# A graph network on one Trainium2 core: constant TensorE products in the third edge stage and in the score stage

## The chip, the cores and the metric

The kernel runs on one core of a Trainium2 chip. The metric is the device time of one execution in microseconds (us). Engines are named as in the profile: PE is TensorE, DVE VectorE, ACT ScalarE, POOL GpSimd, SP SyncE.

## What is computed

Four graph layers, one after the other, on 3125 nodes of 64 features and 103125 edges sorted by their target node. Each layer normalises the nodes, computes something for every edge from its source node, sums over the edges of each target node, and adds the result to the nodes. The parts that matter here are the third layer and the scores of the fourth:

```python
# third layer
he = mlp(edge_z, edge_ln, edge_W, edge_b)           # 64 -> 32 for each edge
msg = concatenate([hn[src], he])                    # 64 for each edge
emb_edge = mlp(msg, red_ln, red_W, red_b)           # layernorm, product, leaky relu
msg_sum = segment_sum(emb_edge, dst) + emb_local
z = msg_sum / (deg + 1)
# fourth layer, its scores
s = leaky_relu(gl[src] + gr[dst])                   # 6 heads of 64
e = einsum('ehf,hf->eh', s, att)
```

## The kernel before

The edges stand in tiles of 128, and 8 tiles are a batch of 1024 edges; 101 batches are in use. The layers are stages that follow one another, each with a loop over the batches in which the engines run side by side and hand work to each other with semaphores, in an order written out by hand. The stages that the change touches are `edge1` (second edge stage, its first instructions only), `edge2` (third edge stage) and `edge3a` (score stage).

**Third edge stage.** Batch number modulo 4 gives its slot. For slots 0, 1 and 2 the 1024 source rows are fetched by GpSimd with 8 indirect DMAs (`Gather.gather`, L892) into the tile `cat` of that slot. For slot 3 (`TAKEN`) nothing is gathered: TensorE selects the rows with one-hot matrices that VectorE makes (`hot`, L1827), in two bursts of 13 products of 128x512 (`choose`, L1683). The first burst is issued in the batch of slot 2, the second in that of slot 3.

For a batch of slots 0 to 2 TensorE (`body`, L1702 to L1750) waits for the gathered rows and for the edge half of `cat` (VectorE, L1853), transposes `cat` into the PSUM tile `catTp` (L1720; in the profile `edge_cat_t_ps`), computes the edge product of the next batch (`edge_part`, L1668), waits until ScalarE has copied `catTp` to SBUF (L1779), multiplies (L1736), and sums the messages of the batch before (`sum_up`, L1676). VectorE adds these sums to the node accumulator (L1875) and makes one-hots between the additions. `by_bank` is another name of `catTp`. The semaphore that counts finished transposes is also the one GpSimd waits for before it starts to gather the next batch of the same slot, four batches further on (`self.free` in `Gather.gather`):

```python
        wait_past(pool, self.free, 2 * t + h - 1)
...
        for j in range(B):
            nc.gpsimd.indirect_dma_start(
```

So one gather of 8 indirect DMAs starts after the transposes of each batch of slots 0, 1 and 2, and none after those of slot 3.

**Score stage.** Here GpSimd gathers all batches in the same manner, again released by the turning of a batch. TensorE does for batch n: `project(n, h, 0)` and `(n, h, 1)` (the first burst of L2040, 8 entries in the timeline), then `turn` of batch n+1 (L2031, L2032, into `hcTp`), `turn_scores` (L2047), and `project` 2 and 3 (second burst). ScalarE copies `hcTp` to SBUF (L2079) once both the turned batch n+1 and the products of batch n are there; VectorE weighs and sums the products (L2133, L2141).

**Start of the second edge stage.** VectorE's `run_marks` reads small PSUM results of TensorE; then its loop begins with a one-hot (L1526). TensorE's first instruction after its last small product is `sums(0, 0, 0)` (L1443).

Of the kernel before, what the change touches and what calls it, by code (L numbers as in the profile page):

```python
# [30 lines left out]
P = 128  # L31
# [133 lines left out]
def behind_one(t, q, m, h):  # L165

    return (t, 1, q, m) if h == 0 else (t + 1, 0, 1 - q, m + q)
# [30 lines left out]
def wait_past(engine, sem, value):  # L198

    if not isinstance(value, int) or value > 0:  # L200
        engine.wait_ge(sem, value)


def over(ap, n):
# [1116 lines left out]
def edge1(nc, k):  # L1321
# [3 lines left out]
    with Ctx(nc, "edge1_") as c:  # L1325
# [12 lines left out]
        rowsTp = c.ps("src_rows_t_ps", [P, ROWS])  # L1338
        row = c.ps("columns_ps", [P, 1, P])
        row_ready = c.sem("columns_in_psum")  # L1340
        ids = c.sb("dst_seq", [P, TILES + 2], I32)
        src = c.sb("src_seq", [P, TILES], I32)
        loop = c.sb("loop", [P, TILES])
# [16 lines left out]
        with nc.Block() as block:  # L1360
# [47 lines left out]
            def _(pe):  # L1408
# [28 lines left out]
                def sums(gi, v, p):  # L1437
                    n, h = GROUP * gi + p, p % 2
                    pe.wait_ge(msg_ready, n + 1)
                    pe.wait_ge(oh_ready, n + 1)  # L1440
                    wait_past(pe, added[B - 1], n - 1)
                    for j in range(B):
                        mm = pe.matmul(sp_[h][j % 2 * D:(j % 2 + 1) * D, j // 2, :], msg[h][:, j, :],  # L1443
                                       oh[h][:, j, :], start=True, stop=True)
                    mm.then_inc(sums_ready, 1)
# [6 lines left out]
                for i in range(3):  # L1452
# [2 lines left out]
                pe.wait_ge(count_ready, 1)  # L1455
                pe.matmul(marks[:, 3 * P:3 * P + 1], carry_t[:, :], k.ident[0:1, 0:1], start=True,
                          stop=True).then_inc(count_turned, 1)
                sums(0, 0, 0)

                def body(u):  # L1460
# [54 lines left out]
            @block.vector  # L1515
            def _(dve):
                def hot(gi, v, u, b):

                    if b == 0:
                        dve.wait_ge(srcb_loaded[v], 16 * (u + 1))  # L1520
                    wait_past(dve, hot_used, NB * gi + b + 1 - RING)
                    dve.tensor_scalar(ring[b % RING][:, :], srcb[v][:, :], k.node_col[:, b:b + 1], None,  # L1522
                                      ALU.is_equal).then_inc(hot_ready, 1)

                def onehot_of(n, h):
                    dve.tensor_tensor(oh[h][:, :, :], over(k.dst_rel[:, bass.ds(n * B, B)], P),  # L1526
                                      row[:, :, :].to_broadcast([P, B, P]), ALU.is_equal).then_inc(oh_ready, 1)

                def add(n, h, j, base):
                    if j > 1:  # L1530
                        dve.wait_ge(added[j - 2], n + 1)
                    else:
                        wait_past(dve, added[B - 2 + j], n)
                    half = slice(j % 2 * D, (j % 2 + 1) * D)
                    acc = k.acc_both[half, bass.ds(base, P)]
                    dve.tensor_tensor(acc, acc, sp_[h][half, j // 2, :], ALU.add).then_inc(added[j], 1)

                dve.wait_ge(high_ready, 1)
                dve.scalar_tensor_tensor(h16[:, :, D:2 * D], k.h[:, :, :], LIFT, h16[:, :, 0:D], ALU.mult,
                                         ALU.subtract).then_inc(prepared, 1)  # L1540
                for b in range(NB):
                    hot(0, 0, 0, b)
                dve.tensor_copy(row[:, 0, :], k.row0[:, :]).then_inc(row_ready, 1)
                dve.wait_ge(row_ready, 1)
                onehot_of(0, 0)
                onehot_of(1, 1)
                dve.memset(k.acc_both, 0.0).then_inc(prepared, 1)
                dve.wait_ge(prepared, 2)
                run_marks(dve, k, ids, src, loop, turn, counts_t, carry_t, carry, marks, Chain(dve, marks_step),
                          seq_loaded, marks_ready, marks_turned, count_ready, count_turned)  # L1550

                def body(u):
                    for v in (0, 1):
                        gi = 2 * u + v
                        for p in range(GROUP):
                            n, h = GROUP * gi + p, p % 2
                            b0, b1 = PART[p]
                            ahead = live(GROUP * gi + GROUP + TAKEN)
                            if not live(n):
                                continue  # L1560
                            dve.wait_ge(sums_ready, n + 1)
                            if live(n + 2):
                                onehot_of(n + 2, h)
                            for j, base in enumerate(batch_starts(nc, k, DVE, n)):
                                add(n, h, j, base)
                                if ahead and b0 + j < b1:
                                    hot(gi + 1, 1 - v, u + v, b0 + j)
                by_groups(dve, body)


def edge2(nc, k, cat, ga, catTp_ready):


    with Ctx(nc, "edge2_") as c:
# [43 lines left out]
        with nc.Block() as block:  # L1618
# [42 lines left out]
            def _(pe):  # L1661
# [10 lines left out]
                def sum_up(n, h):  # L1672
                    pe.wait_ge(msg_ready, n)
                    pe.wait_ge(oh_ready, n)
                    for j in range(B):
                        mm = pe.matmul(sums[:, j, :], msg[h][:, j, :], oh[h][:, j, :], start=True, stop=True)  # L1676
                    mm.then_inc(sums_ready, 1)
# [28 lines left out]
                def body(t, q, m):  # L1706
                    first = isinstance(t, int) and t == 0
                    for h in (0, 1):
# [34 lines left out]
                        if not (first and h == 0):  # L1743
                            if not (first and h == 1):
                                pe.wait_ge(added[B - 1], n)
                            sum_up(n - 1, 1 - h)
                by_parity(pe, body)
                pe.wait_ge(added[B - 1], USED + 1)
                sum_up(USED, 0)
# [170 lines left out]
def edge3a(nc, k):  # L1920
# [3 lines left out]
    with Ctx(nc, "edge3a_") as c:  # L1924
# [25 lines left out]
        with nc.Block() as block:  # L1950
# [67 lines left out]
            def _(pe):  # L2018
# [33 lines left out]
                def body(t, q, m):  # L2052
                    first = isinstance(t, int) and t == 0
                    for h in (0, 1):
                        if not used_batch(t, h):
                            continue
                        n = 2 * t + h + 1
                        pe.wait_ge(hcT_ready, n + 1)
                        project(n, h, 0)
                        project(n, h, 1)  # L2060
                        if used_batch(t, h + 1):
                            tt, hh, qq, mm = behind_one(t, q, m, h)
                            turn(n + 1, hh, tt + 1, qq, mm)
                        if not (first and h == 0):
                            turn_scores(n - 1, 1 - h)
                        project(n, h, 2)
                        project(n, h, 3)
# [427 lines left out]
def build(nc, ins, out):  # L2495
# [15 lines left out]
    with Ctx(nc) as c:  # L2511
# [68 lines left out]
        with Ctx(nc, "layers_") as layers:  # L2580
# [6 lines left out]
            k.before, k.behind, k.kept_before, k.kept_behind, k.times = (  # L2587
                layers.sb(name, [P, TILES]) for name in (
                    "run_before", "run_behind", "kept_before", "kept_behind", "times"))
            k.flags_t = layers.sb("flags_t", [SIDES2, 2, P])  # L2590
            edge1(nc, k)
            with Ctx(nc, "table2_") as shared:
# [89 lines left out]
```

## Time and profile before

| | us |
|---|---|
| median of 3 runs (lowest, highest) | 6671.85 (6656.55, 6678.16) |
| the profiled execution, its time | 6677.32 |
| its span | 6675.1 |
| PE busy | 4704.2 (70%) |
| DVE busy | 4170.2 (62%) |
| POOL busy | 3155.2 (47%) |
| ACT busy | 1888.7 (28%) |
| mean granted TensorE clock | 0.829 of full |
| third edge stage, 3330 to 4576 | 1246.0 |
| score stage, 4671 to 5905 | 1234.0 |

The two stage lines are stretches of the span, in us from its start, with 101 batches each, that is 12.3 and 12.2 us a batch. Busy times are sums over an engine's instructions; the granted clock is the share of the full TensorE clock that the chip granted. A timeline line gives the start, the duration, the engine, the source line, the operation with its output and inputs, how many instructions were put together, and in brackets the idle time of the engine before them with the work that is taken to have ended it.

### The profile page before, as it was taken

To read this page: it belongs to the slowest core of one execution; us is meant where nothing else is said; L and a number is where in the kernel's file an instruction comes from. 1 tells how busy PE (TensorE), PEld (TensorE's weight loads), DVE (VectorE), ACT (ScalarE), POOL (GpSimd) and SP (SyncE) were. 2 spreads that over 40 slices of the span, in tenths; PEclk is the share of its full clock that TensorE was granted. 3 is DMA by queue.
4 is the path that set the end of the run, shared out by engine and by line. 5 is a ranking of instruction groups with operands and counts; after the bars stand their busy time and mean duration, and the time that the engine had idled before them with its cause. 6 is when DMAs were issued, how large, how long until landed. Compare 5 with 4: busy or idle time off the path is not lost. (4 is left out here: it accounts for less than half of the span.)

```text
span 6675.1 us, 100965 instructions
## 1 busy us (share of the span) xinstructions
PE 4704.2 (70%) x28624; PEld 3007.3 (45%) x28624; DVE 4170.2 (62%) x7653; ACT 1888.7 (28%) x6318; POOL 3155.2 (47%) x2946
## 2 busy tenths in 40 slices
PE   3777777777777676667566666663777777739998
PEld 2333333333334333333344554452444444418997
DVE  4454444444446666666666666664666766688997
ACT  1333333333333000000133333331000000016775
POOL 3433343333331655555354454452666666515554
PEclk7778787888888788888677878886999888869999
DMA  3222222222221111111111111111443334411111
GB/s 84 55 54 51 53 56 52 52 51 54 55 54 32 38 38 38 39 39 36 26 41 38 41 40 38 41 40 32 108 111 108 110 110 117 110 49 51 49 49 34
DMA packets 492408, 379.08 MB, mean 57 GB/s; under 512 B 345930, under 2 KB 378971, under 8 KB 492339
## 3 DMA queue, kind: packets, MB, share of 16 engines
q1 hardware_dynamic: 394803, 288.65, 15.3%
q0 software_dynamic: 90560, 83.37, 7.0%
q10 hardware_dynamic: 6976, 6.23, 0.3%
q8 instruction: 33, 0.54, 0.0%
q14 instruction: 36, 0.29, 0.0%
HBM read 341.76 MB, written 36.12 MB: 57 GB/s over the span
## 5 line engine op out<-in xcount | busy, mean ns | idle before, releaser
L1009 POOL DMA_INDIRECT edge_src_rows<-table_wh,edge_gather_idx x806 | 787.1, 977 | 1169.5 <-DVE edge_small L1128 924.6
L1038 PE MATMUL edge_sums_ps<-edge_onehot_src,edge_halves 128*128 128x512 bf16 x4840 | 1048.3, 361 | 302.5 <-issue 296.5
L892 POOL DMA_INDIRECT edge3a_src_rows<-table_h,edge3a_gather_idx x808 | 764.3, 946 | 564.1 <-issue 311.2
L2040 PE MATMUL edge3a_z_ps<-Wz,edge3a_both_ends_t 128*128 128x396 f32 x1616 | 695.3, 579 | 365.2 <-DVE edge3a_terms L2133 315.1
L1114 DVE TENSOR_SCALAR edge_onehot_src<-layer_node_row,edge_src_col,edge_magnitude 128x1568 bf16<-128x1568 f16 x605 | 410.5, 679 | 842.8 <-remote 471.6
L892 POOL DMA_INDIRECT table_cat<-table_hn,table_gather_idx x592 | 599.5, 1013 | 631.6 <-PE edge_cat_t_ps L1720 340.4
L1401 POOL DMA_INDIRECT edge_src_rows<-table_h,edge_gather_idx x608 | 606.9, 998 | 553.9 <-PE edge_msg_ps L1433 190.8
L1038 PEld LDWEIGHTS edge_sums_ps<-edge_onehot_src,edge_halves 128*128 128x128 f16 x4840 | 428.0, 104 | 872.7 <-issue 537.7
L2133 DVE SCALAR_TENSOR_TENSOR edge3a_terms<-edge3a_z_ps,att_z 128x792 f32<-128x792 f32 x404 | 386.0, 977 | 406.1 <-DMA edge_edge_attr<-in_ea 223.9
L2040 PEld LDWEIGHTS edge3a_z_ps<-Wz,edge3a_both_ends_t 128*128 128x128 f32 x1616 | 333.5, 217 | 670.1 <-DVE edge3a_terms L2133 359.6
L2452 PE MATMUL edge3b_sums_ps<-edge3b_onehot,edge3b_weighted 128*128 128x128 f32 x4848 | 572.7, 278 | 6.2 <-DVE layers_accT L2490 4.5
L2452 PEld LDWEIGHTS edge3b_sums_ps<-edge3b_onehot,edge3b_weighted 128*128 128x128 f32 x4848 | 553.5, 193 | 11.8 <-DVE layers_accT L2490 4.7
L1416 PE MATMUL edge_src_rows_t_ps<-edge_onehot_src,edge_h_halves 128*128 128x512 f16 x1300 | 375.1, 431 | 230.4 <-DVE edge_onehot_src L1522 149.2
L2369 POOL TENSOR_TENSOR edge3b_weighted<-edge3b_src_rows,edge3b_alpha 128x1920 f32<-128x1920 f32 x101 | 350.3, 3468 | 344.9 <-DVE edge3b_alpha L2469 251.2
L2418 ACT ACTIVATE edge3b_weighted<-edge3b_src_rows,edge3b_alpha 128x64 f32<-128x64 f32 x1818 | 445.1, 334 | 166.1 <-DVE edge3b_alpha L2469 157.3
L1736 PE MATMUL edge_msg_ps<-rR,edge_cat_t 64*128 64x128 f32 x1616 | 180.7, 388 | 371.8 <-DVE edge_u L1861 255.4
L1066 ACT ACTIVATE edge_dst_rows<-edge_dst_rows_ps 128x390 f32<-128x390 f32 x153 | 70.4, 460 | 1293.1 <-DMA scores_by_head<-setup_zeros 928.5
L2079 ACT ACTIVATE edge3a_both_ends_t<-edge3a_both_ends_t_ps 128x1024 f32<-128x1024 f32 x101 | 103.5, 1024 | 1161.9 <-DMA edge_edge_attr<-in_ea 690.4
L1038 PE MATMUL edge_sums_ps<-edge_onehot_src_act,edge_halves 128*128 128x512 bf16 x1608 | 336.6, 340 | 77.0 <-issue 76.6
L2141 DVE TENSOR_REDUCE edge3a_scores<-edge3a_terms 128x24 f32<-128x1584 f32 x202 | 364.5, 1805 | 7.0
L1023 PE MATMUL edge_dst_rows_ps<-edge_window,edge_onehot_t 128*128 128x65 f32 x1632 | 263.0, 314 | 121.8 <-issue 82.8
L1875 DVE TENSOR_TENSOR layers_accT<-layers_accT,edge_sums_ps 65x128 f32 x808 | 198.7, 280 | 236.7 <-remote 217.7
(372 smaller groups left out, 8320.9 us busy)
## 6 DMA issues: line engine op xcount, KB each, us to landing
edge_dst_row<-in_dst_row SPq DMA_DIRECT2D x102, 512.0 KB
edge3a_dst_row<-in_dst_row SPq DMA_DIRECT2D x102, 512.0 KB
edge_window<-table_wh SPq DMA_DIRECT2D x816, 32.5 KB
edge3a_window<-table_h SPq DMA_DIRECT2D x816, 32.0 KB
edge_edge_attr<-in_ea SPq DMA_DIRECT2D x101, 256.0 KB
kept_rows<-edge3a_src_rows SPq DMA_DIRECT2D x101, 256.0 KB
edge3b_src_rows<-kept_rows SPq DMA_DIRECT2D x101, 256.0 KB
edge_edge_attr<-in_ea SPq DMA_DIRECT2D x101, 128.0 KB
```

The lines of the kernel that those rows point to most:

```text
L892: nc.gpsimd.indirect_dma_start(self.slot(b, j), None, self.table[:, :], bass.IndirectOffsetOnAxis(ap=self.idx[b][:, j:j + 1], axis=0)).the ...
L1009: nc.gpsimd.indirect_dma_start(g[q][:, j, :], None, k.t_wh[:, :], bass.IndirectOffsetOnAxis(ap=idx[q][:, j:j + 1], axis=0)).then_inc(gathe ...
L1038: mm = pe.matmul(acc[:, i, 0:w], halves[q][:, j, a, :, :].rearrange("p h d -> p (h d)"), hot[:, o:o + w], start=first and a == 0, stop=False)
L1114: dve.tensor_scalar(slot_v(q, j)[:, :], k.node_row[:, :], col[q][:, j:j + 1], mag[q][:, j:j + 1], ALU.is_equal, ALU.mult).then_inc(hot_v, 1)
L1401: nc.gpsimd.indirect_dma_start(g[p][:, j, :], None, k.t_h[:, :], bass.IndirectOffsetOnAxis(ap=idx[p][:, j:j + 1], axis=0)).then_inc(gather ...
L1416: mm = pe.matmul(rowsTp[:, o:o + 512], h16[:, b, :], ring[b % RING][:, o:o + 512], start=(b == 0), stop=(b == NB - 1))
L2040: mm = pe.matmul(zp[q % 2][:, i, 0:H * ZH], hcT[h][:, j * P:(j + 1) * P], k.Wz[:, :], start=True, stop=True)
L2133: dve.scalar_tensor_tensor(terms[:, 2 * q:2 * q + 2, :], zp[q % 2][:, :, 0:H * ZH], 0.0, rows_over(k.att_z[:, :], 2), ALU.max, ALU.mult).t ...
L2141: dve.tensor_reduce(scs[h][:, :, j:j + B // 2].rearrange("p h b -> p b h"), terms[:, j:j + B // 2, :].rearrange("p b (h f) -> p b h f", h= ...
L2369: return engine.tensor_tensor(hp[h][:, a:b, :, :], rows, weights, ALU.mult)
L2418: w = act.activation(hp[h][:, j, a, :], st[h][:, j, :], ACT.Copy, scale=al[h][:, a, j:j + 1])
L2452: mm = pe.matmul(sums[j % 4][:, i, :], hp[h][:, j, 2 * i:2 * i + 2, :].rearrange("p a d -> p (a d)"), oh[h][:, j, :], start=True, stop=True)
```

## The change

A function `spin` issues products of a constant fp16 matrix of 128x128 with a constant fp16 matrix of 128x512. Nobody reads the results. The third edge stage issues 10 of them at the end of each batch, except the batch of slot 2, into the bank of `catTp` (76 times). The score stage issues 6 between `project(n, h, 1)` and `turn` of the next batch, into the first bank of `hcTp` (100 times). The constants are a new SBUF tile `fill`, written once by VectorE at the start of the second edge stage, where TensorE waits for that with a new semaphore.

```diff
+def spin(pe, k, out, times):
+
+    for _ in range(times):
+        pe.matmul(out, k.fill[:, 0:P], k.fill[:, :], start=True, stop=True)
...
+        marks_free = c.sem("marks_read")
...
                 pe.matmul(marks[:, 3 * P:3 * P + 1], carry_t[:, :], k.ident[0:1, 0:1], start=True,
                           stop=True).then_inc(count_turned, 1)
+                pe.wait_ge(marks_free, 1)
                 sums(0, 0, 0)
...
                           seq_loaded, marks_ready, marks_turned, count_ready, count_turned)
+                dve.memset(k.fill[:, :], 1.0).then_inc(marks_free, 1)
...
                             if not (first and h == 1):
                                 pe.wait_ge(added[B - 1], n)
                             sum_up(n - 1, 1 - h)
+                        if b != TAKEN - 1:
+                            spin(pe, k, by_bank, 10)
...
                         project(n, h, 1)
                         if used_batch(t, h + 1):
                             tt, hh, qq, mm = behind_one(t, q, m, h)
+                            spin(pe, k, hcTp[:, 0:512], 6)
                             turn(n + 1, hh, tt + 1, qq, mm)
...
+            k.fill = layers.sb("fill", [P, 512], F16)
```

In the changed kernel the lines of the third edge stage are numbered 9 higher and those of the score stage 11 higher; the new products have line L207. The instructions of ACT, POOL and SP stand as they did.

TensorE in the loop of the third edge stage, before: the end of one batch, the next batch's transposes into `edge_cat_t_ps`, and that batch up to its sums.

```order
L1736 MATMUL edge_msg_ps<-rR,edge_cat_t 128x128 x8
L1676 MATMUL edge_sums_ps<-edge_onehot,edge_msg 65x128 x8
L1716 REGISTER_ALU
L1717 ISA
L1720 MATMUL edge_cat_t_ps<-ident,table_cat 128x128 x4
L1668 MATMUL edge_he_ps<-eR,edge_edge_attr 128x96 x8
L1736 MATMUL edge_msg_ps<-rR,edge_cat_t 128x128 x8
L1676 MATMUL edge_sums_ps<-edge_onehot,edge_msg 65x128 x8
L1717 REGISTER_ALU
L1720 MATMUL edge_cat_t_ps<-ident,table_cat 128x128 x4
```

The same place with the change.

```order
L1745 MATMUL edge_msg_ps<-rR,edge_cat_t 128x128 x8
L1685 MATMUL edge_sums_ps<-edge_onehot,edge_msg 65x128 x8
L207 MATMUL edge_cat_t_ps<-layers_fill 128x512 x10
L1725 REGISTER_ALU
L1726 ISA
L1729 MATMUL edge_cat_t_ps<-ident,table_cat 128x128 x4
L1677 MATMUL edge_he_ps<-eR,edge_edge_attr 128x96 x8
L1745 MATMUL edge_msg_ps<-rR,edge_cat_t 128x128 x8
L1685 MATMUL edge_sums_ps<-edge_onehot,edge_msg 65x128 x8
L207 MATMUL edge_cat_t_ps<-layers_fill 128x512 x10
```

The 10 products stand between a batch's sums and the wait (ISA) for the next batch's gathered rows, ahead of its transposes.

TensorE in the score stage, before: the end of one turning, the second burst of a batch and the first of the next (4 products each, in one line), and the next turning.

```order
L2032 MATMUL edge3a_both_ends_t_ps<-ident,edge3a_src_rows 64x128
L2047 MATMUL edge3a_scores_t_ps<-ident,edge3a_scores 48x128
L2040 MATMUL edge3a_z_ps<-Wz,edge3a_both_ends_t 128x396 x8
L2031 MATMUL edge3a_both_ends_t_ps<-edge3a_onehot_t,edge3a_window 64x128
L2032 MATMUL edge3a_both_ends_t_ps<-ident,edge3a_src_rows 64x128
L2031 MATMUL edge3a_both_ends_t_ps<-edge3a_onehot_t,edge3a_window 64x128
```

The same place with the change.

```order
L2043 MATMUL edge3a_both_ends_t_ps<-ident,edge3a_src_rows 64x128
L2058 MATMUL edge3a_scores_t_ps<-ident,edge3a_scores 48x128
L2051 MATMUL edge3a_z_ps<-Wz,edge3a_both_ends_t 128x396 x8
L207 MATMUL edge3a_both_ends_t_ps<-layers_fill 128x512 x6
L2042 MATMUL edge3a_both_ends_t_ps<-edge3a_onehot_t,edge3a_window 64x128
L2043 MATMUL edge3a_both_ends_t_ps<-ident,edge3a_src_rows 64x128
L2042 MATMUL edge3a_both_ends_t_ps<-edge3a_onehot_t,edge3a_window 64x128
```

The 6 products stand behind the first burst and ahead of the turning of the next batch.

## Rows read from the trace of the kernel before

**Rows 1.** Busy time by stretch: third edge stage, then score stage. Columns in the first line.

```profile
core 0: us, PE busy (x) PEld busy (x) DVE busy (x) ACT busy (x) POOL busy (x), PEclk, DMA share, GB/s
3330.00:4576.00 1246.00, 804.28 (x5998) 619.75 (x5998) 809.25 (x2162) 459.64 (x3501) 591.65 (x585) 0.80 0.16 38
4671.00:5905.00 1234.00, 899.85 (x5016) 526.93 (x5015) 857.37 (x803) 118.08 (x200) 733.39 (x776) 0.90 0.40 110
```

**Rows 2.** Waits of the third edge stage: who waited, for whom, us, times, longest.

```profile
POOL table_cat L892 <- PE edge_cat_t_ps L1720: 340.4, 26, 15.2
```

**Rows 3.** Timeline, TensorE: start, us, engine, line, operation; idle before in brackets.

```profile
3928.04 1.96 PE L1676 MATMUL edge_sums_ps<-edge_onehot,edge_msg 128*65 128x128 f32 x16
...
3930.60 0.66 PE L1720 MATMUL edge_cat_t_ps<-ident,table_cat 128*128 128x128 f32 x4 [0.60 <-DVE table_cat L1853]
...
3938.27 3.19 PE L1676 MATMUL edge_sums_ps<-edge_onehot,edge_msg 128*65 128x128 f32 x16
...
3941.29 0.60 PE L1720 MATMUL edge_cat_t_ps<-ident,table_cat 128*128 128x128 f32 x4
```

**Rows 4.** Timeline, TensorE, the batch of slot 1 that follows.

```profile
3954.49 0.60 PE L1720 MATMUL edge_cat_t_ps<-ident,table_cat 128*128 128x128 f32 x4
```

**Rows 5.** Timeline, GpSimd: gathers of the same stretch.

```profile
3932.05 1.67 POOL L892 DMA_INDIRECT table_cat<-table_hn,table_gather_idx  x1 [15.09 <-PE edge_cat_t_ps L1720]
...
3941.53 0.95 POOL L892 DMA_INDIRECT table_cat<-table_hn,table_gather_idx  x1 [0.30 <-issue]
...
3944.73 0.95 POOL L892 DMA_INDIRECT table_cat<-table_hn,table_gather_idx  x1 [2.25 <-issue]
...
3957.21 0.95 POOL L892 DMA_INDIRECT table_cat<-table_hn,table_gather_idx  x1 [2.16 <-PE edge_cat_t_ps L1720]
```

**Rows 6.** Timeline, VectorE, same stretch.

```profile
3944.75 0.28 DVE L1875 TENSOR_TENSOR layers_accT<-layers_accT,edge_sums_ps 65x128 f32 x1 [4.51 <-remote]
```

**Rows 7.** Timeline, TensorE, the same place one cycle later.

```profile
3987.13 2.67 PE L1676 MATMUL edge_sums_ps<-edge_onehot,edge_msg 128*65 128x128 f32 x16
```

**Rows 8.** Timeline, GpSimd, one cycle later: first and last gather of eight.

```profile
3980.93 1.67 POOL L892 DMA_INDIRECT table_cat<-table_hn,table_gather_idx  x1 [13.70 <-PE edge_cat_t_ps L1720]
...
3991.43 0.95 POOL L892 DMA_INDIRECT table_cat<-table_hn,table_gather_idx  x1 [0.31 <-issue]
```

**Rows 9.** Timeline, VectorE, one cycle later.

```profile
3994.74 0.28 DVE L1875 TENSOR_TENSOR layers_accT<-layers_accT,edge_sums_ps 65x128 f32 x1 [5.62 <-remote]
```

**Rows 10.** Timeline, TensorE: a second selection burst, partly at half clock.

```profile
3919.15 4.60 PE L1683 MATMUL edge_cat_t_ps<-edge_onehot_src,edge_node_parts 128*128 128x512 f16 x13 [1.98 <-DVE edge_src_rows_t L1837]
```

**Rows 11.** Timeline, TensorE: a second selection burst at full clock.

```profile
3668.99 2.98 PE L1683 MATMUL edge_cat_t_ps<-edge_onehot_src,edge_node_parts 128*128 128x512 f16 x13 [1.36 <-DVE edge_src_rows_t L1837]
```

**Rows 12.** Timeline, ScalarE, score stage.

```profile
4915.32 1.02 ACT L2079 ACTIVATE edge3a_both_ends_t<-edge3a_both_ends_t_ps 128x1024 f32<-128x1024 f32 x1 [11.04 <-DMA edge_edge_attr<-in_ea]
...
4927.40 1.02 ACT L2079 ACTIVATE edge3a_both_ends_t<-edge3a_both_ends_t_ps 128x1024 f32<-128x1024 f32 x1 [10.90 <-PE edge3a_z_ps L2040]
...
4939.45 1.02 ACT L2079 ACTIVATE edge3a_both_ends_t<-edge3a_both_ends_t_ps 128x1024 f32<-128x1024 f32 x1 [10.88 <-DMA edge_edge_attr<-in_ea]
```

**Rows 13.** Timeline, TensorE, score stage: the two bursts of a batch, the first of the next.

```profile
4916.48 4.62 PE L2040 MATMUL edge3a_z_ps<-Wz,edge3a_both_ends_t 128*128 128x396 f32 x8 [4.30 <-DVE edge3a_terms L2133]
...
4923.14 2.93 PE L2040 MATMUL edge3a_z_ps<-Wz,edge3a_both_ends_t 128*128 128x396 f32 x8
...
4928.56 2.92 PE L2040 MATMUL edge3a_z_ps<-Wz,edge3a_both_ends_t 128*128 128x396 f32 x8 [2.50 <-DVE edge3a_terms L2133]
```

**Rows 14.** Timeline, GpSimd, score stage: last gather of eight.

```profile
4924.80 0.95 POOL L892 DMA_INDIRECT edge3a_src_rows<-table_h,edge3a_gather_idx  x1 [0.30 <-issue]
```

**Rows 15.** Timeline, VectorE, start of the second edge stage.

```profile
2168.44 2.83 DVE L1547 MEMSET layers_accT<- 128x3328 f32 x1 [0.64 <-issue]
...
2191.93 1.22 DVE L1526 TENSOR_TENSOR edge_onehot<-dst_rel,edge_columns_ps 128x1024 f32<-128x1024 f32 x1
```

**Rows 16.** Timeline, TensorE, start of the second edge stage.

```profile
2188.24 1.97 PE L1443 MATMUL edge_sums_ps<-edge_onehot,edge_msg 128*64 128x128 f32 x32
```
## The prediction

> **What bounds the kernel now.** I read the windows of the two changed stages first. Neither is full of TensorE work: in the third edge stage TensorE is busy 804.28 of 1246 us, VectorE 809.25, GpSimd 591.65, at a granted clock of 0.80; in the score stage 899.85, 857.37 and 733.39 of 1234, at 0.90 [rows 1]. So waits set the time, and the question is whose. The table of waits shows GpSimd waiting for the transposes of L1720 340.4 us in 26 waits, up to 15.2 us each [rows 2]. 26 is the number of groups of four batches: GpSimd pauses once in each, where the batch of slot 3 brings it no gather. So I read one such cycle in the timelines.
>
> TensorE ends the sums of slot 3 at 3929.99 (3928.04 + 1.96) and starts the transposes of slot 0 at 3930.60, after only 0.60 us for the edge half made by VectorE [rows 3]. They end at 3931.26, and GpSimd starts its 8 gathers 0.79 later, at 3932.05 [rows 5]. That pair sets the pace of what follows: the last of the 8 ends at 3942.48 (3941.53 + 0.95) [rows 5]. TensorE's next sums ended at 3941.46 (3938.27 + 3.19) [rows 3], but VectorE, which adds them, resumes only at 3944.75, after 4.51 us idle [rows 6]; the transposes of slot 1 ended at 3941.89 [rows 3], and GpSimd, free since 3942.48, starts the next gather at 3944.73 [rows 5]. Both start some 2.3 us after the last gather's end. One cycle later the gathers run from 3980.93 and end at 3992.38 (3991.43 + 0.95) [rows 8], TensorE's sums end at 3989.80 [rows 7], and VectorE resumes at 3994.74 [rows 9], 2.36 after the gathers' end and 4.94 after TensorE's. The two distances to the gathers agree (2.27, 2.36), those to TensorE do not (3.29, 4.94). I choose the reading that, while a gather of 8 is running, what TensorE finishes is seen by the others only behind the last gather. The chain then goes: transposes of slot 0, gather, release, next gather. TensorE's clock is no part of it.
>
> **The change, part by part.** *One product* of the new kind is 128x512 in fp16, as the 13 of L1683. At full clock 13 take 2.98 us [rows 11]; with 0.38 for the last one to drain (my estimate, between 0 and the 0.66 that all 4 transposes take [rows 3]) each adds (2.98 - 0.38) / 12 = 0.217. So 10 take 2.17 and 6 take 1.30. Partly at half clock 13 take 4.60 [rows 10], so 10 are at most 3.54.
>
> *Third edge stage, slot 3, 25 times.* The 10 products start where the sums end, 3929.99, and end at 3932.16. TensorE idled 0.60 there; the transposes move by 2.17 - 0.60 = +1.57, and GpSimd's pause grows by it, 13.70 to 15.09 us already [rows 5, 8], so it had long been ready. 25 x 1.57 = **+39**. Bounds: all of 2.17 (25 x 2.17 = +54) if the cover of 0.60 is VectorE waiting in turn, and 0 if the later batches of the cycle return it.
>
> *Slot 0, 25 times.* The transposes of slot 1 ended at 3941.89, the release came some 2.0 later. 2.17 more fit to within 0.2; I take +0.1 each, **+2**, from 0 to +5. Name the cover: it is the gather, and it moves with the slot 3 delay.
>
> *Slot 1, 25 times.* Transposes end at 3955.09 (3954.49 + 0.60, no idle time ahead) [rows 4], GpSimd starts at 3957.21, by then idle 2.16 [rows 5]. With 2.17 they end at 3957.26, and with the 0.79 of above GpSimd starts at 3958.05: +0.84. In cycles where the sums are shorter (the 2.67 of rows 7 against 3.19 in rows 3) part of it fits. I take +0.4 each, **+10**, from 0 to +21.
>
> *Slot 2* has no products. Its batch and that of slot 3 hold the two selection bursts, which stand on the chain: GpSimd is in its long pause then. The second takes 4.60 in one cycle and 2.98 in another, 1.62 less [rows 10, 11]. I counted it slow in 13 of 25 cycles; if the products made all of them fast, 13 x 1.62 = -21. But the burst comes a whole batch after the nearest products, with 1.98 and 1.36 us of idle time directly ahead of it in the two cases, and that wait, for VectorE, is not shortened. I take **0**, from -21 to +19 (the other 12 slow).
>
> *VectorE in slot 0* makes its one-hots beside the first gather (1.67 instead of 0.95 [rows 5, 8]). It moves along; 0.
>
> *Score stage, 100 times.* The batch with a first burst of 4.62 and the next with 2.92 [rows 13] take 12.08 and 12.05 from one copy by ScalarE to the next [rows 12]. So 1.7 us of TensorE time moves the period by 0.03: here too the gathers hold it. The last of 8 ends at 4925.75 (4924.80 + 0.95) [rows 14], ScalarE copies at 4927.40 [rows 12], 1.65 later, while TensorE's second burst had ended at 4926.07 (4923.14 + 2.93) [rows 13]. The slack is 1.33 in the slow case and 1.7 more in the fast one; 1.30 fits in both, just. **0**, from -2 (the 0.03) to +9 (some 10 bursts that are slower still, 0.9 each, an estimate). The cover is the gather; without it 6 products would cost their whole length.
>
> *Second edge stage, once.* TensorE issued its 32 entries of two batches from 2188.24 [rows 16]; now they wait for VectorE, whose first one-hot starts at 2191.93 [rows 15], plus the memset: 2.83 us for 3328 columns [rows 15] gives 0.44 for 512. What TensorE does there, half of 1.97, is 0.99. **+1**, from 0 to +2.
>
> Sum: 39 + 2 + 10 + 0 + 0 + 1 = **+52** on the profiled execution's 6677.3, 6729. The median of the runs is 5.5 lower, so I predict 6724.
>
> **Where a rule speaks the other way.** The rows show TensorE idle in every batch of the score stage (4.30 and 2.50 ahead of the first burst) and the same burst at 4.62 or 2.92 [rows 13]: clock 1.2 GHz for part of it, then 2.4. The Trainium skill, page "TensorE: Matmul & The Clock Gate", says that idle gaps between bursts cost clock and that TensorE should be kept fed. The trace agrees that the clock is lost behind idle time; it doesn't agree that time is lost by it here, since 4.62 and 2.92 give one period. By the rule the change should be faster, which is rival C.
>
> **The rivals.**
> A, the forecast: the products of slot 3 delay the chain, the rest is covered. Chance 0.62.
> B, returned: the products raise the clock enough that the selection bursts all take 2.98 (-21), and slot 1 costs nothing; 39 + 2 + 1 - 21 = +21 with the rest at 0, and about +10 if the first burst gains too. Against it: the idle time ahead of the bursts. Around 6687. Chance 0.17.
> C, faster: TensorE, not the gathers, releases the batches. Then a first burst of 2.92 instead of 4.62 in some 60 score batches is 60 x 1.7 = -102, with -21 for the selection bursts and +39 + 1: -83, 6589. It decides at one point: whether ScalarE's copy follows TensorE's second burst or the last gather. Rows 12 to 14 speak for the gather. A lesser form, the selection bursts alone gaining in both batches with the delay of slot 3 swallowed, gives -30, 6642. Chance 0.10.
> D, slower by much: the 6 products don't fit in the 1.33 us, or what TensorE posts late misses one release and waits for a later one. 100 x 1.30 = +130 with the +52: 6854. Against it the slack, for it that it is only just enough. Chance 0.07.
> E, the products do not raise the clock at all (constant data, or the throttle sees them otherwise). The sum of A hardly changes, as no term of it is a gain, but 10 products at half clock take up to 3.54 instead of 2.17: 25 x 1.37 = +34 more, 6758. Chance 0.04.
>
> **How the numbers follow.** A measurement of this kernel can tell about 0.3% from no change, 20 us. A has its own range, 6690 to 6760, from its bounds; a few us of it lie under 6692. Faster by over 0.3% is C: 0.10. Within 0.3% is most of B and the low edge of A: 0.17. Slower: 0.73. The range of 8 in 10 takes A and B with E: 6670 to 6765; C and D stay out.
>
> **What would show it.** Right: in the third edge stage the 10 products (L207) behind the sums of slot 3, the transposes of slot 0 starting some 1.6 us later against VectorE's edge half, GpSimd's waits for L1729 some 40 us longer in sum, the stage 1298 instead of 1246 us; the score stage at 1234 still, with a higher granted clock. Wrong: if the score stage gets shorter, TensorE set its period; if the third stage stays at 1246, the delay of slot 3 was returned within the cycle, and my reading of the release falls; if the score stage grows by 60 us or more, the slack was no slack.

## The result: 6719 us, and the profile after

| | before | after |
|---|---|---|
| median of 5 runs each (lowest, highest), us | 6671.85 (6650.61, 6678.16) | 6719.28 (6705.97, 6737.4) |
| span of the profiled execution, us | 6675.1 | 6717.1 |
| third edge stage: first L1736 (after: L1745) to last, us | 1244.6 | 1271.2 |
| score stage: first L2040 (after: L2051) to last, us | 1234.8 | 1257.1 |
| mean granted clock | 0.829 | 0.843 |

The ratio is 1.0078, 95% interval 1.0057 to 1.0098: slower by 47 us. The prediction was 6724, in the range 6670 to 6765. The sum came out; its terms did not all. Of the 42 us of the two spans 26.6 lie in the third edge stage, where +51 was forecast, and 22.3 in the score stage, where 0 was. The rest, -7, is what other stretches differ by.

One thing has to be said before the experiments. They ran on three chips (numbers 4, 7 and 15), and there the kernel before takes 5230 us, not 6672 (5224 to 5242 in 73 runs). The record names no chip for the runs of the table, so it isn't known whether another chip, another setting or the recording of the traces makes the difference. The program is the same. "First condition" (6672 us) and "second condition" (5230 us) name the two below, and the difference between them turned out to be the most instructive part of this case.

The windows of the changed kernel's two stages, in the columns of their first line, stand against [rows 1].

```profile
core 0: us, PE busy (x) PEld busy (x) DVE busy (x) ACT busy (x) POOL busy (x), PEclk, DMA share, GB/s
3327.00:4598.00 1271.00, 957.81 (x6736) 689.94 (x6736) 806.31 (x2158) 460.94 (x3500) 585.44 (x584) 0.83 0.16 38
4690.00:5947.00 1257.00, 1040.59 (x5616) 568.82 (x5615) 857.28 (x804) 117.97 (x200) 731.37 (x776) 0.94 0.40 108
```

TensorE is busier (958 instead of 804 us, 1041 instead of 900), the clock is up by 0.03 and 0.04, and both stages are longer. The higher clock did not make either stage shorter here.

The same place of the third edge stage as in [rows 3], TensorE's timeline with the change:

```profile
3932.49 1.96 PE L1685 MATMUL edge_sums_ps<-edge_onehot,edge_msg 128*65 128x128 f32 x16
...
3934.29 2.32 PE L207 MATMUL edge_cat_t_ps<-layers_fill 128*128 128x512 f16 x10
...
3936.44 0.60 PE L1729 MATMUL edge_cat_t_ps<-ident,table_cat 128*128 128x128 f32 x4
...
3947.65 0.60 PE L1729 MATMUL edge_cat_t_ps<-ident,table_cat 128*128 128x128 f32 x4
```

The 10 products start behind the sums of slot 3, and the transposes come 1.99 us behind the end of the sums (3934.45), not 0.60. GpSimd, which answers to [rows 5], starts 0.79 later, as before:

```profile
3937.83 0.94 POOL L898 DMA_INDIRECT table_cat<-table_hn,table_gather_idx  x1 [15.21 <-PE edge_cat_t_ps L1729]
...
3946.97 0.94 POOL L898 DMA_INDIRECT table_cat<-table_hn,table_gather_idx  x1 [0.30 <-issue]
...
3950.25 0.94 POOL L898 DMA_INDIRECT table_cat<-table_hn,table_gather_idx  x1 [2.34 <-issue]
```

Its pause behind the last gather is 2.34 us, where [rows 5] has 2.25. In the table of waits its line has grown from 340.4 us in 26 waits to 407.6 in 44 [rows 2]:

```profile
POOL table_cat L898 <- PE edge_cat_t_ps L1729: 407.6, 44, 16.7
```

In the score stage something new stands in TensorE's timeline. First the burst, the 6 products, and the second burst, which is in pieces:

```profile
4927.89 4.62 PE L2051 MATMUL edge3a_z_ps<-Wz,edge3a_both_ends_t 128*128 128x396 f32 x8 [1.66 <-DVE edge3a_terms L2145]
...
4932.34 1.46 PE L207 MATMUL edge3a_both_ends_t_ps<-layers_fill 128*128 128x512 f16 x6
...
4935.84 0.93 PE L2051 MATMUL edge3a_z_ps<-Wz,edge3a_both_ends_t 128*128 128x396 f32 x2
...
4937.26 1.21 PE L2051 MATMUL edge3a_z_ps<-Wz,edge3a_both_ends_t 128*128 128x396 f32 x2 [0.49 <-issue]
...
4938.69 4.38 PE L2051 MATMUL edge3a_z_ps<-Wz,edge3a_both_ends_t 128*128 128x396 f32 x12 [0.21 <-issue]
```

Then the gathers (first and last of eight) and ScalarE's copies of the same batch:

```profile
4927.39 0.94 POOL L898 DMA_INDIRECT edge3a_src_rows<-table_h,edge3a_gather_idx  x1 [2.58 <-DMA edge_edge_attr<-in_ea]
...
4936.12 0.94 POOL L898 DMA_INDIRECT edge3a_src_rows<-table_h,edge3a_gather_idx  x1 [0.30 <-issue]
```

```profile
4926.72 1.02 ACT L2091 ACTIVATE edge3a_both_ends_t<-edge3a_both_ends_t_ps 128x1024 f32<-128x1024 f32 x1 [11.54 <-PE edge3a_z_ps L2051]
...
4938.99 1.02 ACT L2091 ACTIVATE edge3a_both_ends_t<-edge3a_both_ends_t_ps 128x1024 f32<-128x1024 f32 x1 [11.10 <-PE edge3a_z_ps L2051]
```

The second burst, 8 entries in 2.93 us in [rows 13], starts at 4935.84 and hands out 2 entries, then 2 more 1.4 us later, and the rest runs into the next first burst (12 entries in one row). ScalarE copies 1.93 us behind the last gather (4937.06), where it was 1.65 [rows 12, 14], and the batch takes 12.27 us instead of 12.05 to 12.08.

Does time or a number run out here? An entry is one instruction of those that a line of the timeline puts together. A batch of the kernel before has exactly 50 product entries (16 in the two bursts, 32 in the turning, 2 for the scores); with the change it has 56. Over the whole stage with the change, 78 of 86 gathers of eight have a gap of over 0.15 us in TensorE's work, in 76 of them after 47 to 53 entries counted from the start of the gathers, and that can be 7.0, 8.5 or 9.9 us after it. Batches with the gap take 12.34 us in the median, the eight without it 12.15 (a few of over 13 us left out). In the kernel before only 8 of 85 have such a gap, after 48 to 51 entries, and a batch takes 12.13. So a number fits better than a time: TensorE gets some 50 entries ahead while gathers run, and behind that an entry comes every 0.7 to 0.8 us. 0.2 us in nine of ten batches is some 18 of the stage's 22 us (an estimate from these medians). This is a reading of the traces; no run made in this condition varied the number. And the number isn't the same everywhere: in the third edge stage with the change TensorE begins 54 to 61 entries before its gap in 21 gathers, and 62 without one in 22.

What the prediction took for the rule, that everything TensorE finishes during a gather is seen only behind it, is not what these traces show. ScalarE, TensorE and ScalarE again, third edge stage of the kernel before, with gathers running from 3932.05 to 3942.48 [rows 5]:

```profile
3932.38 0.22 ACT L1756 ACTIVATE edge_squares<-edge_he_ps 128x64 f32<-128x64 f32 x1 [0.48 <-PE edge_he_ps L1668]
...
3936.26 2.08 PE L1736 MATMUL edge_msg_ps<-rR,edge_cat_t 64*128 64x128 f32 x16 [3.92 <-DVE edge_u L1861]
...
3938.37 0.23 ACT L1756 ACTIVATE edge_squares<-edge_msg_ps 128x64 f32<-128x64 f32 x1 [3.91 <-PE edge_msg_ps L1736]
...
3943.99 0.60 ACT L1779 ACTIVATE edge_cat_t<-edge_cat_t_ps 128x512 f32<-128x512 f32 x1 [2.74 <-DMA edge_gather_idx<-in_src_t]
```

TensorE ends L1736 at 3938.34, and ScalarE takes the result up 0.03 us later, in the middle of the gathers. Over the stage ScalarE does so while the gathers still run in 71 of 72 cases, in 27 of them within 0.1 us and in the others up to 3.7 us late. VectorE in the score stage, with gathers from 4916.04 to 4925.75 and the first burst ending at 4921.10 [rows 13, 14]:

```profile
4919.10 0.98 DVE L2133 SCALAR_TENSOR_TENSOR edge3a_terms<-edge3a_z_ps,att_z 128x792 f32<-128x792 f32 x1
...
4921.13 0.98 DVE L2133 SCALAR_TENSOR_TENSOR edge3a_terms<-edge3a_z_ps,att_z 128x792 f32<-128x792 f32 x1 [0.97 <-issue]
```

What comes late is what TensorE finishes later in a gather. Its sums end 5 to 10 us into one, and VectorE starts to add them only 2.04 to 2.45 us behind the last gather in all 51 cases. The transposes that end at 3941.89 reach ScalarE at 3943.99, 1.51 us behind the gathers. These late results are the ones that the prediction's chain uses, so its terms could be right although its rule is too wide.

At the start of the second edge stage, VectorE and then TensorE:

```profile
2162.34 2.83 DVE L1555 MEMSET layers_accT<- 128x3328 f32 x1 [0.65 <-issue]
...
2186.13 0.48 DVE L1559 MEMSET layers_fill<- 128x512 f16 x1 [0.17 <-DVE layers_times L1324]
```

```profile
2186.67 3.68 PE L1450 MATMUL edge_sums_ps<-edge_onehot,edge_msg 128*64 128x128 f32 x32 [4.29 <-DVE layers_fill L1559]
```

The memset takes 0.48, where 0.44 was estimated. From the first memset to the sums there are 24.33 us now and were 19.80 [rows 15, 16], and the 32 entries take 3.68 instead of 1.97, right behind 4.29 us in which TensorE idled. VectorE's first one-hot comes 2.86 us later, not 1.

### The profile page after: what moved, and what is told of

It is laid out like the page before. It is cut to its first block and busy times, and to the rows that moved or that the text cites. A ratio compares the mean times of both kernels' runs of the same rounds, so it can differ in the third digit from the quotient of the medians.

```text
span 6717.1 us, 103685 instructions
## 1 busy us (share of the span) xinstructions
PE 4989.6 (74%) x29984; PEld 3116.7 (46%) x29984; DVE 4170.8 (62%) x7654; ACT 1890.7 (28%) x6318; POOL 3142.5 (47%) x2946
## 5 line engine op out<-in xcount | busy, mean ns | idle before, releaser
L898 POOL DMA_INDIRECT table_cat<-table_hn,table_gather_idx x592 | 594.1, 1004 | 664.9 <-PE edge_cat_t_ps L1729 407.6
L2051 PE MATMUL edge3a_z_ps<-Wz,edge3a_both_ends_t 128*128 128x396 f32 x1616 | 702.3, 559 | 239.8 <-issue 115.9
L2051 PEld LDWEIGHTS edge3a_z_ps<-Wz,edge3a_both_ends_t 128*128 128x128 f32 x1616 | 316.1, 207 | 580.6 <-issue 297.4
L1745 PE MATMUL edge_msg_ps<-rR,edge_cat_t 64*128 64x128 f32 x1616 | 170.0, 370 | 261.4 <-DVE edge_u L1872 191.1
```

Source lines behind the costliest of these rows:

```text
L898: nc.gpsimd.indirect_dma_start(self.slot(b, j), None, self.table[:, :], bass.IndirectOffsetOnAxis(ap=self.idx[b][:, j:j + 1], axis=0)).the ...
L2051: mm = pe.matmul(zp[q % 2][:, i, 0:H * ZH], hcT[h][:, j * P:(j + 1) * P], k.Wz[:, :], start=True, stop=True)
```

## The experiments

Eleven kernels ran, all in the second condition, each with a profile, beside the kernel before on the same chip. Where a kernel has products, the fill tile and the new wait are in it too.

### The kernel before again

> The kernel before, unaltered, for its trace. If it takes 5236 us again: in the third edge stage the gathers of slots 0, 1 and 2 follow each other 1.25 us apart without a pause, and VectorE takes up TensorE's sums within 0.1 us of their end, while a gather runs. If it takes 6672: as in the profile of before, with pauses of 2.2 us between the gathers.

5230.64 us, ratio 1.0004 (0.9994 to 1.0015). Its windows for the two stages:

```profile
core 0: us, PE busy (x) PEld busy (x) DVE busy (x) ACT busy (x) POOL busy (x), PEclk, DMA share, GB/s
2365.00:3384.00 1019.00, 717.77 (x5990) 579.97 (x5988) 805.56 (x2159) 463.08 (x3500) 579.54 (x584) 0.88 0.20 47
3450.00:4457.00 1007.00, 816.73 (x5016) 509.17 (x5016) 854.86 (x803) 117.82 (x200) 750.16 (x795) 0.97 0.51 135
```

1019 us where the first condition has 1246, and 1007 where it has 1234. The timelines tell why. TensorE, GpSimd and VectorE:

```profile
2927.03 1.96 PE L1676 MATMUL edge_sums_ps<-edge_onehot,edge_msg 128*65 128x128 f32 x16
...
2935.23 2.08 PE L1736 MATMUL edge_msg_ps<-rR,edge_cat_t 64*128 64x128 f32 x16 [3.92 <-DVE edge_u L1861]
...
2937.23 3.22 PE L1676 MATMUL edge_sums_ps<-edge_onehot,edge_msg 128*65 128x128 f32 x16
...
2946.98 3.45 PE L1676 MATMUL edge_sums_ps<-edge_onehot,edge_msg 128*65 128x128 f32 x16 [0.24 <-issue]
...
2955.16 2.98 PE L1683 MATMUL edge_cat_t_ps<-edge_onehot_src,edge_node_parts 128*128 128x512 f16 x13
```

```profile
2931.03 1.67 POOL L892 DMA_INDIRECT table_cat<-table_hn,table_gather_idx  x1 [8.49 <-PE edge_cat_t_ps L1720]
...
2940.49 0.95 POOL L892 DMA_INDIRECT table_cat<-table_hn,table_gather_idx  x1 [0.30 <-issue]
...
2941.74 1.11 POOL L892 DMA_INDIRECT table_cat<-table_hn,table_gather_idx  x1 [0.30 <-issue]
```

```profile
2941.31 0.28 DVE L1875 TENSOR_TENSOR layers_accT<-layers_accT,edge_sums_ps 65x128 f32 x1 [2.10 <-PE edge_sums_ps L1676]
```

An indirect DMA takes the same 0.94 and the eight the same 10 us. But the ninth, at 2941.74, follows the eighth with no pause, and VectorE adds TensorE's sums at 2941.31, in the middle of a gather, 0.86 us after their end (2940.45). (The expectation said within 0.1; in the whole stage it is 0.79 to 0.89.) In the first condition it added them only 2.27 us behind the last gather [rows 5, 6]. So in the first condition the late results of TensorE are held past the gathers, and here they are not: 72 of the 73 results of L1736 that end during gathers are taken up within 0.04 us, too. What makes the conditions differ stays open. One more difference is on record: the traces of the first two kernels hold 41213 and 40249 updates of semaphores, those of the eleven runs here 98389 to 101974. So the recording itself ran differently in the first condition. Whether that is a cause of the held results or only goes with them, no run shows.

### The change itself, and its two stages apart

> The change itself, unaltered, beside the four partial kernels. In those the kernel before took 5236.6 us instead of 6671.9, and its gathers followed each other without the pauses of 2.2 us that the profile of before shows. If this state holds here too: the products of slots 0 and 1 gave -34 us, those of slot 3 +14, the score stage -2; the whole -13 to -25 us, ratio 0.995 to 0.998. If the state of the first profiles is back (before at 6672): +47 us.

5221.87 us against 5229.83, ratio 0.9984 (0.9975 to 0.9993): in this condition the change is a little faster.

```diff
                             tt, hh, qq, mm = behind_one(t, q, m, h)
-                            spin(pe, k, hcTp[:, 0:512], 6)
                             turn(n + 1, hh, tt + 1, qq, mm)
```

> The change without the 6 products of the score stage. The two profiles already show the third edge stage 26.6 us longer and the score stage 22.3 us longer. If both are real and separate: about +25 us against before, score stage at 1235 us again. By the sums of the prediction (third stage +51, score stage 0): +51 us, and the score stage's 22 us would have been chance of one execution.

0.9976 (0.9965 to 0.9987), third edge stage 1014.8 us against 1018.8, score stage 1007.5 both.

```diff
-                        if b != TAKEN - 1:
-                            spin(pe, k, by_bank, 10)
```

> The change without the 10 products of the third edge stage. Theory run-ahead: while 8 gathers run, TensorE can finish only some 50 product entries before it is held (the batch of before has exactly 50), so 6 more are held to about 0.7 us each: score stage 1257 us, +22 us in all, the batch at 12.3 instead of 12.1 us. By the prediction's slack (6 x 0.217 fits in 1.33 us): 1235 us, no change.

0.9996 (0.9987 to 1.0005), score stage 1007.6 us. So the score stage's 22 us is not there, and all that the change does here is in the third edge stage. The question of theory run-ahead couldn't be put in this condition: nothing is held, so nothing runs out.

### Slots apart

The same line with `if b == TAKEN:`, `if b < TAKEN - 1:`, `if b == 0:` and `if b == 1:`, none in the score stage.

> Third edge stage with the 10 products only behind the batch of slot 3, none in the score stage. By the chain as predicted the transposes of slot 0 come 1.39 us later (1.99 instead of 0.60 behind the sums) in 25 cycles: up to +35 us, and about +25 if the shorter first gather (10.08 instead of 10.43) gives part back. If the delay of slot 3 is swallowed and slots 0 and 1 cost: 0.

> Third edge stage with the 10 products only behind the batches of slots 0 and 1, none in the score stage. By the prediction +12 us (0.1 and 0.4 us in 25 cycles each). If it is the run-ahead that costs here too (16 + 16 + 10 + 4 + 16 entries in a gather): +15 to +30 us. If slot 3 alone costs: 0.

> Third edge stage with the 10 products only behind the batch of slot 0. In the partial runs the sums of slot 1 took 3.44 us without products and 1.93 in most cycles with those of slots 0 and 1, and the batch 6.98 instead of 8.49. Theory clock: it is the products of slot 0, the nearest ones ahead, that bring these sums to full clock, so this kernel has the whole -34 us. Rival: those of slot 1 of the same cycle count as much, and this one has less than half. (If before takes 6672 here: +3 us by the prediction's term for slot 0.)

> Third edge stage with the 10 products only behind the batch of slot 1. Theory clock: they come behind the sums of slot 1, ahead of slot 2, whose bursts ran at full clock anyway: 0, or a few us more, since the transposes of slot 2 are 2.2 us later. Rival: this one has the -34 us. (If before takes 6672 here: +10 us by the prediction's term for slot 1.)

| products behind the sums of | ratio (95%) | third edge stage, us | slot 0 to 1 | 1 to 2 | 2 to 3 | 3 to 0 |
|---|---|---|---|---|---|---|
| none | 1.0004 (0.9994 to 1.0015) | 1018.8 | 10.33 | 8.48 | 12.83 | 9.29 |
| slot 3 | 1.0027 (1.0014 to 1.0039) | 1060.5 | 9.88 | 8.81 | 14.76 | 9.30 |
| slots 0, 1 | 0.9938 (0.9925 to 0.9951) | 992.4 | 10.28 | 7.42 | 12.83 | 9.29 |
| slot 0 | 0.9996 (0.9986 to 1.0005) | 1018.0 | 10.16 | 7.43 | 14.10 | 9.30 |
| slot 1 | 0.9998 (0.9988 to 1.0007) | 1018.9 | 10.33 | 8.47 | 12.83 | 9.29 |
| slots 0, 1, 3 | 0.9976 (0.9965 to 0.9987) | 1014.8 | 10.04 | 8.48 | 12.97 | 9.29 |

The last four columns are mean times from one slot's L1736 to the next, in the profiled execution, without its first and last cycles. (The kernel with slot 3 spreads most, 5231 to 5268 us; its profile was of the slowest. The whole change has the same third edge stage as the last line and took 1008.1 us there, so differences of some 7 us between two profiles say nothing.) Three things are to be seen. Slot 3 to slot 0 is 9.3 us in all of them, products or not, though the transposes in it move by 1.39: TensorE stood idle 3.92 us behind them and now stands 2.59. So the delay that the prediction priced costs nothing where nothing is held. Second, the expectation for slot 0 alone was wrong by itself and half right in its reason. Its products do bring the sums of slot 1 to full clock (slots 0 and 1 together, then slot 0 alone):

```profile
2883.31 2.32 PE L207 MATMUL edge_cat_t_ps<-layers_fill 128*128 128x512 f16 x10
...
2888.60 1.16 PE L1745 MATMUL edge_msg_ps<-rR,edge_cat_t 64*128 64x128 f32 x16 [1.47 <-DVE edge_u L1872]
...
2890.01 1.93 PE L1685 MATMUL edge_sums_ps<-edge_onehot,edge_msg 128*65 128x128 f32 x16 [0.24 <-issue]
...
2896.67 2.98 PE L1692 MATMUL edge_cat_t_ps<-edge_onehot_src,edge_node_parts 128*128 128x512 f16 x13
```

```profile
2908.83 1.93 PE L1685 MATMUL edge_sums_ps<-edge_onehot,edge_msg 128*65 128x128 f32 x16 [0.24 <-issue]
...
2914.40 1.33 PE L1745 MATMUL edge_msg_ps<-rR,edge_cat_t 64*128 64x128 f32 x16 [2.14 <-DVE edge_u L1872]
...
2915.67 4.44 PE L1692 MATMUL edge_cat_t_ps<-edge_onehot_src,edge_node_parts 128*128 128x512 f16 x13
```

1.93 us where the kernel before has 3.45 (2946.98 above), and the batch 1.5 us shorter in most cycles. But with slot 0 alone the first selection burst of slot 2 then takes 4.44 instead of 2.98 (it is long in 16 of 25 cycles): the half clock has moved from a batch where it cost 1.5 us to one where it costs 1.5. Only with the products of slot 1 behind it does the clock last through slot 2, and the two together give -26 us in the stage, while each alone gives nothing. Third, slot 3 alone moves the half clock onto slot 2 in the same way:

```profile
2890.28 2.08 PE L1745 MATMUL edge_msg_ps<-rR,edge_cat_t 64*128 64x128 f32 x16 [2.14 <-DVE edge_u L1872]
...
2892.29 5.06 PE L1692 MATMUL edge_cat_t_ps<-edge_onehot_src,edge_node_parts 128*128 128x512 f16 x13
```

2.08 and 5.06 us, where it was 1.16 and 2.98. That is its +41 us in this profile.

### Gathers and products in the score stage

```diff
-        for j in range(B):
+        for j in range(B if isinstance(m, int) and m == 0 else self.later):
```

with `later=6` in the score stage, and the counts that wait for the gathers changed to match. From the fifth batch on this kernel leaves out the fetching of two of the eight tiles of a batch, so its scores are not those of the program.

> The kernel before, where the score stage fetches only 6 of the 8 tiles of a batch from the fifth batch on (the other two keep old rows; their scores are those of other edges). If GpSimd's gathers set the period of the score stage, as the prediction says: 2 x 1.25 x 97 = -240 us, the batch at 9.6 us where it was 12.1, or at 8.9, where TensorE or VectorE become the bound, if it was 10.0. If TensorE or VectorE set it: no change.

5075.82 us, 0.9707 (0.9688 to 0.9725); score stage 854.9 instead of 1007.5, 1.5 us a batch and not 2.5. The gathers do set the period in this condition, and another bound stands close behind at some 8.5 us. It is VectorE: it is busy 834.65 of the 845 us from 3455 to 4300, with four L2133 of 0.98, two L2141 of 1.80 and a one-hot of 1.21 in each batch.

```diff
-                            spin(pe, k, hcTp[:, 0:512], 6)
+                            spin(pe, k, hcTp[:, 0:512], 12)
```

> Score stage with 12 products a batch instead of 6, none in the third edge stage. In the state where before takes 5230 us the gathers follow each other without a pause (8 x 1.25 = 10.0 us a batch) and TensorE has 10.0 - 8.0 = 2 us left: 12 x 0.217 = 2.6 us don't fit wholly, at most +0.6 x 100 = +60 us, 0 if the four buffers take it up. In the state of the first profiles (before at 6672) 62 entries stand against a run-ahead of some 50: 12 held entries instead of 6, +45 us or more.

1.0056 (1.0039 to 1.0073), score stage 1040.2 instead of 1007.5.

```profile
3709.89 5.69 PE L2049 MATMUL edge3a_z_ps<-Wz,edge3a_both_ends_t 128*128 128x396 f32 x16
...
3715.42 2.75 PE L207 MATMUL edge3a_both_ends_t_ps<-layers_fill 128*128 128x512 f16 x12
...
3718.10 0.32 PE L2040 MATMUL edge3a_both_ends_t_ps<-edge3a_onehot_t,edge3a_window 128*64 128x128 f32 x1
...
3720.22 4.03 PE L2049 MATMUL edge3a_z_ps<-Wz,edge3a_both_ends_t 128*128 128x396 f32 x11
```

TensorE is busy without a gap (1029.94 of the 1030 us from 3460 to 4490), and the period is 10.33 us (3709.89 to 3720.22) instead of 10.0: 100 x 0.33 = 33 us, as measured. 6 products fit, 12 are 0.33 us too long.

### Products where TensorE waits

If the clock is what counts, the products should stand where TensorE is idle and nothing is behind them. That is after ScalarE's copy, before the wait for VectorE's scaling.

```diff
                         pe.wait_ge(catT_ready, n)
+                        if b != TAKEN:
+                            spin(pe, k, by_bank, (12, 10, 6)[b])
                         if not (first and h == 0):
                             pe.wait_ge(u_sc, n - 1)
...
-                        if b != TAKEN - 1:
-                            spin(pe, k, by_bank, 10)
...
-                            spin(pe, k, hcTp[:, 0:512], 6)
```

> Third edge stage with 12, 10 and 6 products in the batches of slots 0, 1 and 2, not behind the sums but between the wait for ScalarE's copy and the wait for VectorE's scaling, where TensorE stands idle 3.92, 3.63 and 2.14 us; none in the score stage. There they are ahead of nothing that waits (2.6, 2.2 and 1.3 us). Theory clock, in the state with before at 5230 us: the two half-clock stretches of a cycle (10.3 of 40.9 us) go, the product of slot 0 falls from 2.08 to 1.16 and the sums of slots 0 and 1 from 3.22 and 3.44 to 1.96: 1.5 x 25 = -37 us by slot 1 alone, -90 if slot 0's 2.1 us are on the chain too. Rival: the chain there is VectorE's, -34 us as with slots 0 and 1 behind the sums, or less. In the state with before at 6672: no delay of the transposes, so 0, or more time if the run-ahead of some 50 entries is used up sooner.

5148.7 us against 5231.99, 0.9836 (0.9823 to 0.985): faster than both kernels, by 83 us. The third edge stage takes 932.8 us instead of 1018.8, and its granted clock is 1.0 from end to end.

```profile
2891.10 2.76 PE L207 MATMUL edge_cat_t_ps<-layers_fill 128*128 128x512 f16 x12
...
2895.00 1.16 PE L1747 MATMUL edge_msg_ps<-rR,edge_cat_t 64*128 64x128 f32 x16 [1.14 <-DVE edge_u L1872]
...
2896.49 1.93 PE L1685 MATMUL edge_sums_ps<-edge_onehot,edge_msg 128*65 128x128 f32 x16 [0.33 <-issue]
...
2899.86 2.33 PE L207 MATMUL edge_cat_t_ps<-layers_fill 128*128 128x512 f16 x10
...
2904.96 1.93 PE L1685 MATMUL edge_sums_ps<-edge_onehot,edge_msg 128*65 128x128 f32 x16 [0.33 <-issue]
```

Every piece is at its short length (1.16, 1.93), TensorE still has 1.14, 1.27 and 0.65 us of idle time in front of L1747 in slots 0, 1 and 2, so no product delays anything, and slots 0 and 1 take 8.47 and 6.97 us instead of 10.33 and 8.48. 25 x (1.86 + 1.51) = 84 us. Theory clock holds in its larger form. The Trainium skill, page "TensorE: Matmul & The Clock Gate", section "Why this matters for your kernels", wants idle gaps between bursts avoided. Here the trace agrees (clock 0.88 to 1.0), and the time follows. This kernel wasn't run in the first condition, where nothing shows that the clock is on the chain.

## Why the prediction was right, and where it was not

- **What bounds the kernel** (the gathers and the release behind them, not TensorE's clock): right for the condition it was read in, as far as the traces tell. The clock rose in both stages and the time did too. It is a property of that condition, though: in the second one the same program has the clock on its chain in slots 0 and 1 of the third edge stage, which is rival C's reading in part.
- **The rule behind it** ("while a gather of 8 is running, what TensorE finishes is seen by the others only behind the last gather"): too wide. Results that end in the first 6.4 us of a gather are mostly taken up while it runs (3938.34 to 3938.37 above); the sums and transposes that end later are late, and they are what the terms for slots 0 and 1 rest on.
- **Slot 3, +39**: the transposes moved by 1.39 and not 1.57, in every cycle. The first product starts 0.16 before the sums are drained, which the sum had left out. From the first gather of one cycle to that of the next it is 50.10 us before and 51.23 after (means of 22 cycles, as all that follow), +1.13, that is +28 in all. The stretch that holds the delay, from the third gather to the first of the next cycle, grew by 1.13 (24.70 to 25.83): 0.26 of the 1.39 came back in it. The second selection burst shows about as much, 3.87 to 3.67; it is at 4.4 to 4.7 us in 12 of 25 cycles before (the prediction counted 13) and in 9 with the change.
- **Slot 0, +2**: it was -0.32 (12.76 to 12.44 from the first to the second gather). The step "it moves along; 0" failed. VectorE's one-hots no longer run beside the first indirect DMA, which takes 0.94 and not 1.67 [rows 5]. This gain belongs to the delay of slot 3.
- **Slot 1, +10**: +0.33 a cycle (12.64 to 12.97), near the +0.4 forecast.
- **Slot 2, 0**: right within 0.2 us a cycle.
- **Score stage, 0**: wrong, +22. The step "1.30 fits in both, just" compared times of TensorE alone. The trace shows TensorE stopped behind some 50 entries, whenever that is, so what ran out looks like a number and not time: the 50 of before mostly fit, 56 don't. It is rival D's place with a sixth of its price, since only the last entries are held.
- **Second edge stage, +1**: +2.9 until VectorE's first one-hot. The sum left out that TensorE, idle for 4.29 us, then takes 3.68 us for the 32 entries and not 1.97.

So the forecast hit 6719 with 6724 because a term of +51 that was 24 too large stood beside one of 0 that was 22 too small. The signs that it named failed in part as well: the third edge stage was to be at 1298 us and is at 1271, the score stage was to stay at 1234 and is at 1257. The direction rests on the one term that was read from a row and came out (the delayed transposes), the exactness on chance.

## What to carry to other kernels

Before products are added to keep the clock up, find in the trace what ends the wait in front of the slow burst, and put them where the engine idles with nothing queued behind them: 28 products in four batches gave 83 us there, while behind the sums 20 gave 32, 30 gave 12, and 10 cost 14. Test such fillers together as well as one by one, because a stretch of half clock that is driven out of one batch can fall onto the next. And measure the kernel before again beside every experiment before a change of 1% is called a gain or a loss; here the sign differed between two conditions of the same program.

## What was not expected of the hardware

- Two conditions for one program: 6672 us and 5230 us, 28% apart, with each indirect DMA at 0.94 us in both. In the slower one the results that TensorE finishes late in a gather reach ScalarE 1.5 to 1.9 us and VectorE 2.0 to 2.5 us behind its end, while most of the earlier ones are taken up during it.
- In the slower one TensorE gets some 50 product entries ahead in most batches of the score stage and is then held to one in 0.7 to 0.8 us; in the third edge stage it gets to 54 to 62. Whether it is entries, instructions or results that are counted, and whether the recording of the trace, which every run here had and which kept less than half of the semaphore updates in this condition, plays a part, stays open.
- The half clock moves: 10 products in slot 0 shorten slot 1 by 1.05 us and lengthen slot 2 by 1.27 in the mean.
